# Turning half of x on VectorE and through memory, instead of on TensorE, in the first stage of a fused block on one core

## Chip, core and metric

One core of one Trainium2 chip runs the whole kernel in one launch. The metric is the device time of that core in microseconds (us), the median of several runs. TensorE (PE) is the matrix engine, VectorE (DVE), ScalarE (ACT) and GpSimd (POOL) are the other compute engines, and SyncE (SP) issues the kernel's DMAs.

## What is computed

The reference is one block: a normalised input goes into gated linear attention with 32 heads and 8 groups of keys and values, and behind that stands a small feed-forward part. What matters here is the start:

```
x = L0_attn_hidden_states                                # 4 batches x 512 tokens x 512
h = _layernorm(x, axis=-1)
q = (h @ Wq.T).reshape(B, L, H, D)
k = (h @ Wk.T).reshape(B, L, KVH, D)
v = (h @ Wv.T).reshape(B, L, KVH, D)
...
dt = jax.nn.softplus(h @ Win.T + dt_bias)
```

Every product contracts over the 512 features. TensorE contracts over the partitions, and x arrives with its tokens there, so each normalised tile of 128 tokens by 512 features has to be turned once, so that its features lie on the partitions. Float32 products are made of three passes, high by high, high by low and low by high, so each turned tile is also split into a high and a low part.

## The kernel before

The program has three stages. The change is in the first, `norm_stage`, which takes the first 130 us of the span. There are 16 tiles of 128 tokens, numbered i, four to a batch. `n_xin` holds them all, `n_xn` has three slots (`NORM_SLOTS`) of normalised tiles, and `n_pt` two banks of PSUM that take a turned tile, tile i in bank i % 2. The parts of the turned x stay in `shared`, for the whole program, the high part (index 0) beside the low one (index 1).

For each tile, the engines do this, all in an order written by hand, one in-order list for each engine:

- DVE: `normalise(i)` (L312) writes `n_xn`. It waits until TensorE has turned the tile three before it (`xt_done`). `low_part(i)` (L317) subtracts the saved high part from the bank and writes the low part.
- PE: `turn(i)` (L466) is four transposes of 128 by 128, by the identity, into `n_pt`. `values(v)` (L88, here with outputs `p_tok` and `p_kept`) makes the values of tile v, 12 matmuls of 128x512, and `dt_rows(b)` (L477) is 12 more for each batch, into `n_pdt`. `values(v)` waits for the low part of its tile and for the copy of the tile of values two before it (`v_set`), since there are two banks.
- ACT: `halves(i)` (L391) copies the bank into the high part, and `save_v(v)` (L403) copies a tile of values out of PSUM. The weights' high parts (L395) stand between them, those of the second half of Wv behind `halves(9)` and those of Wk behind `halves(11)`.
- SP: after the loads come `store_v(v)` (L216) for each tile of values, to `v_scratch` in HBM, each waiting for `save_v(v)`. The loads of the first group of Wq (L241) stand behind the eighth of them.

PE's loop over i has `turn(i)`, then `values(i - 2)`, and `dt_rows` behind the values of tiles 3, 7 and 11. After the loop come the values of tile 14, the last `dt_rows` and the values of tile 15, and then those of the second half of Wv (16 and on). ACT's loop is `halves(i)`, then weights if any, then `save_v(i - 2)`. DVE's loop from tile 4 on is `normalise(i)`, `low_part(i - 1)`, with the statistics of four tiles before `normalise` at i = 6 and 10.

The stage ends with decay tables, the first keys and queries, and more values; none of that is moved.

Of the kernel before, what the change touches and what calls it, by code (L numbers as in the profile page):

```python
# [25 lines left out]
ALU = mybir.AluOpType  # L26
# [5 lines left out]
P = 128  # L32
# [87 lines left out]
def norm_stage(nc, io, keep):  # L120
# [7 lines left out]
    with ExitStack() as ctx:  # L128
# [45 lines left out]
        const_set, acol_set = sem("n_const_set"), sem("n_acol_set")  # L174
# [4 lines left out]
        gg_set, G_set, wexp_set, eg_set = sem("n_gg_set"), sem("n_G_set"), sem("n_wexp_set"), sem("n_eg_set")  # L179
        dt_set, dt_up_set, ln_dt_set, ln_dt_min = sem("n_dt_set"), sem("n_dt_up_set"), sem("n_ln_dt_set"), sem("n_ln_dt_min")  # L180
        row_set = [sem(f"n_row_set{k}") for k in range(TAB)]
# [9 lines left out]

        TABLES = 4

        V_LAG, TABLES_AT = 2, 10

# [12 lines left out]
        def _(sp):  # L208
# [87 lines left out]
        def _(dve):  # L296
# [11 lines left out]
            def normalise(i):  # L308
                dve.wait_ge(rstd_set, 1 + next(j for j, (c0, c1) in enumerate(TOGETHER) if i < c1))
                if i >= NORM_SLOTS:  # L310
                    dve.wait_ge(xt_done, i - NORM_SLOTS + 1)
                dve.tensor_scalar(xn[:, i % NORM_SLOTS, :], xin[:, i, :], mv[:, i, 0:1], rstd[:, i:i + 1],  # L312
                                  ALU.subtract, ALU.mult).then_inc(xn_set, 1)

            def low_part(i):
                dve.wait_ge(xt_saved, i + 1)
                dve.tensor_tensor(x_part(1, i), pt[i % 2][:, :, :], x_part(0, i).bitcast(F32), ALU.subtract).then_inc(lo_set, 1)  # L317
# [27 lines left out]
            for i in range(NC, NT):  # L345
# [3 lines left out]
                low_part(i - 1)  # L349
            low_part(NT - 1)  # L350
# [16 lines left out]
            dve.wait_ge(acol_set, 1)  # L367
            dve.tensor_scalar(gg[:, :], dt[:, :], hcol[:, 2:3], -1.0, ALU.mult, ALU.mult).then_inc(gg_set, 1)
            dve.wait_ge(gg_set, 1)
# [9 lines left out]
            dve.tensor_tensor(rows[T_BIAS][:, :], ln_dt[:, :], G[:, :], ALU.subtract).then_inc(row_set[T_BIAS], 1)  # L379
            dve.wait_ge(wexp_set, 1)  # L380
            dve.tensor_tensor(rows[T_W][:, :], dt[:, :], wexp[:, :], ALU.mult).then_inc(row_set[T_W], 1)
# [5 lines left out]
        def _(act):  # L387
            def halves(i):

                act.wait_ge(xt_done, i + 1)  # L390
                act.activation(x_part(0, i), pt[i % 2][:, :, :], ACT.Copy).then_inc(xt_saved, 1)  # L391
# [5 lines left out]
            def save_v(v):  # L397
# [3 lines left out]
                if v in (NT - 2, NT - 1, NT, NT + 1):  # L401
                    act.wait_ge(xt_done, NT)
                act.activation(v_place(v), pv[v % 2][:, :], ACT.Copy).then_inc(v_set, 1)  # L403

            for i in range(NT):
# [9 lines left out]
                if i == 11:  # L415
                    w_high(wk, 0, k_in, 16)
                    act.wait_ge(small_in, 16 * 2 * B)
                    act.activation(hcol[:, 2:3], hcol[:, 1:2], ACT.Exp).then_inc(acol_set, 1)
# [1565 lines left out]
```

## Time and profile before

| | us |
|---|---|
| median of 3 runs | 1765.15 (1765.02 to 1765.41) |
| the profiled execution, its own time | 1765.26 |
| its span | 1763.4 |
| TensorE busy | 1738.6 (99%) |
| VectorE, GpSimd, ScalarE busy | 1271.4, 851.6, 715.1 |
| TensorE, VectorE, ScalarE, GpSimd busy from 20 to 40 us | 20.0, 10.4, 6.8, 3.2 |
| the same from 40 to 60 us | 20.0, 7.1, 7.4, 7.5 |
| share of the 16 DMA engines busy from 20 to 40 and 40 to 60 us | 0.44, 0.43 |

In the rows below a start is in us from the start of the span, the second number is the duration, and the brackets hold the idle time of the engine just before, with what ended it. Matmuls are pipelined, so the distance from one start to the next says what one costs, and not its duration. What lies outside the span (1765.26 less 1763.4) is 1.9 us.

### The profile page before, as it was taken

The numbers are of one execution on the slowest core, as the hardware profiler recorded it, in microseconds if no ns is written. First come the engines' busy times: TensorE is split into PE (matmuls) and PEld (weight loads), VectorE is DVE, ScalarE is ACT, GpSimd is POOL, SyncE is SP. The second block draws the span as 40 slices with busy tenths as digits, with TensorE's granted clock in tenths as the row PEclk, the third lists the DMA queues.
The fourth block names the chain that finished last, engine by engine and source line by source line (L and its number), as shares of the span: only waits on it lengthen the run. The fifth ranks groups of instructions, "written<-read, shape, count | busy, mean of one in ns | idle before, by whom it ended". The sixth has DMA issues, their size and how long they took to land. (4 is left out here: it accounts for less than half of the span.)

```text
span 1763.4 us, 27984 instructions
## 1 busy us (share of the span) xinstructions
PE 1738.6 (99%) x8744; PEld 1468.0 (83%) x8744; DVE 1271.4 (72%) x2353; ACT 715.1 (41%) x2232; POOL 851.6 (48%) x862
## 2 busy tenths in 40 slices
PE   7999999999999999999999999999999999999998
PEld 6788888888888888888888888888778888888886
DVE  5327899998989989889999998998864333333332
ACT  3424444444455444544445444544652212121111
POOL 3126676667667666767666666766401101010101
PEclk9999999999999999999999999999999999999999
DMA  6235323433433333332433333333572323232321
GB/s 208 91 100 146 91 73 118 116 93 112 120 87 118 118 86 111 114 102 77 118 117 90 111 120 88 118 88 105 195 253 76 99 78 102 76 103 74 104 73 47
DMA packets 145985, 190.31 MB, mean 108 GB/s; under 512 B 9136, under 2 KB 79792, under 8 KB 145840
## 3 DMA queue, kind: packets, MB, share of 16 engines
q1 hardware_dynamic: 145840, 188.58, 35.6%
q8 instruction: 66, 1.08, 0.3%
q14 instruction: 79, 0.65, 0.2%
HBM read 141.89 MB, written 46.66 MB: 107 GB/s over the span
## 5 line engine op out<-in xcount | busy, mean ns | idle before, releaser
L117 POOL TENSOR_TENSOR q<-raw_wo_early 128x512 f32<-128x512 f32 x128 | 165.3, 1291 | 195.8 <-DVE raw_wo_early L109 195.6
L88 PE MATMUL p_proj<-shared,wq_hi 128*128 128x512 f32 x744 | 244.5, 389 | 0.0
L1135 ACT ACTIVATE square<-p_y 128x128 f32<-128x128 f32 x512 | 134.2, 277 | 220.1 <-PE p_y L849 218.7
L1877 POOL TENSOR_TENSOR var<-mv,eps 128x1 f32<-128x1 f32 x16 | 3.0, 190 | 402.6 <-DVE mv L1727 402.6
L849 PE MATMUL p_y<-v_tok,probs 128*128 128x128 f32 x1024 | 183.0, 276 | 0.0
L1007 DVE SCALAR_TENSOR_TENSOR z<-p_y,srstd,gate 128x128 f32<-128x128 f32 x512 | 143.7, 343 | 51.6 <-issue 34.5
L1110 ACT ACTIVATE probs<-g_row,stab 128x128 f32<-128x128 f32 x512 | 164.3, 407 | 24.2 <-POOL g_row L1244 24.1
L88 PE MATMUL p_kept<-wg_hi,shared 128*128 128x512 f32 x560 | 173.1, 390 | 0.0
L1258 POOL TENSOR_TENSOR xw_lo<-xw_raw,xw_hi 128x512 fp32r<-128x512 f32 x96 | 131.0, 1364 | 86.0 <-ACT xw_hi L1151 86.0
L88 PEld LDWEIGHTS p_proj<-shared,wq_hi 128*128 128x128 f32 x744 | 139.7, 188 | 30.4 <-DVE raw_wo_early L109 1.2
L1266 POOL TENSOR_TENSOR srstd<-svar,mhalf 128x4 f32<-128x4 f32 x128 | 157.7, 1232 | 10.0
L88 PE MATMUL p_proj<-wg_hi,shared 128*128 128x512 f32 x528 | 162.5, 389 | 0.0
L849 PEld LDWEIGHTS p_y<-v_tok,probs 128*128 128x128 f32 x1024 | 151.0, 193 | 2.5
L848 PE MATMUL p_y<-state,qs 128*128 128x128 f32 x768 | 149.3, 276 | 2.3 <-DVE qs L972 2.3
L88 PE MATMUL p_proj<-shared,wq_lo 128*128 128x512 f32 x372 | 144.8, 389 | 0.0
L1409 DVE TENSOR_TENSOR wq_lo<-w_raw,wq_hi 128x1024 fp32r<-128x1024 f32 x62 | 75.8, 1223 | 83.8 <-ACT wq_hi L1404 83.8
L848 PEld LDWEIGHTS p_y<-state,qs 128*128 128x128 f32 x768 | 122.0, 193 | 7.9 <-issue 3.0
L88 PEld LDWEIGHTS p_kept<-wg_hi,shared 128*128 128x128 f32 x560 | 104.6, 188 | 21.4
L1151 ACT ACTIVATE xw_hi<-xw_raw 128x512 fp32r<-128x512 f32 x96 | 60.7, 632 | 151.7 <-POOL xw_raw L1254 125.3
L88 PEld LDWEIGHTS p_proj<-wg_hi,shared 128*128 128x128 f32 x528 | 99.1, 188 | 21.0
L1254 POOL TENSOR_TENSOR xw_raw<-v_tok,stab 128x512 f32<-128x512 f32 x96 | 110.0, 1146 | 0.1
L88 PE MATMUL p_kept<-wg_lo,shared 128*128 128x512 f32 x280 | 109.1, 390 | 0.0
(244 smaller groups left out, 4395.3 us busy)
## 6 DMA issues: line engine op xcount, KB each, us to landing
g_row<-g_scratch SPq DMA_DIRECT2D x128, 256.0 KB, 5.1
z_scratch<-z_st SPq DMA_DIRECT2D x256, 128.0 KB
w_raw<-z_scratch SPq DMA_DIRECT2D x62, 512.0 KB, 6.7
e_row<-e_scratch SPq DMA_DIRECT2D x96, 256.0 KB, 4.1
w_raw<-in_wq_t SPq DMA_DIRECT2D x16, 512.0 KB, 7.3
w_raw<-in_wg_t SPq DMA_DIRECT2D x16, 512.0 KB, 5.6
v_tok<-v_scratch SPq DMA_DIRECT2D x32, 256.0 KB, 2.9
v_scratch<-n_xin SPq DMA_DIRECT2D x20, 256.0 KB, 2.3
```

The lines of the kernel that those rows point to most:

```text
L88: mm = pe.matmul(out, lhs[a], rhs[e], start=(i == 0 and j == 0), stop=(i == len(pairs) - 1 and j == 2))
L117: pool.tensor_tensor(out, keep["rope_a"][:, s, :], keep["rope_b"][:, s, :], ALU.add).then_inc(keep["roped"], 1)
L848: pe.matmul(p_y[c % 2][:, h, :], qs[:, h, :], state[:, c % 2, h, :], start=True, stop=False)
L849: mm = pe.matmul(p_y[c % 2][:, h, :], probs[:, c % 2, h, :], v_tok[:, b % 2, c, :], start=(c == 0), stop=True)
L1007: zz = dve.scalar_tensor_tensor(z[:, h, :], p_y[c % 2][:, h, :], srstd[:, c, h:h + 1], gate[:, c % 2, h * D:(h + 1) * D], ALU.mult, ALU.mult)
L1110: e = act.activation(probs[:, c % 2, h, :], g_row[:, c % 2, h, :], ACT.Exp, bias=stab[:, b % 2, c, T_BIAS, h:h + 1])
L1135: s = act.activation(square[:, h, :], p_y[c % 2][:, h, :], ACT.Square, scale=2.0 / float(np.sqrt(D)), accum_out=ssum[:, c, h:h + 1])
L1151: act.activation(xw[0][:, :, :], xw_raw[:, :, :], ACT.Copy).then_inc(xw_hi_set, 1)
L1254: pool.tensor_tensor(xw_raw[:, :, :], v, w, ALU.mult).then_inc(xw_raw_set, 1)
L1258: pool.tensor_tensor(xw[1][:, :, :], xw_raw[:, :, :], xw[0][:, :, :].bitcast(F32), ALU.subtract).then_inc(xw_set, 1)
L1266: pool.tensor_tensor(srstd[:, c, :], svar[:, c, :], mhalf[:, :], ALU.pow).then_inc(srstd_set, 1)
L1409: dve.tensor_tensor(by_half(keep["z_lo"][slot]), raw_z(keep, raw_slot), by_half(keep["z_hi"][slot].bitcast(F32)), ALU.subtract).then_inc(k ...
```

## The change

Tiles 8 to 15 (batches 2 and 3) are not turned by TensorE. For them:

- DVE normalises the tile into the PSUM bank `n_pt` instead of `n_xn` and then turns each of its 4 by 16 blocks of 32x32 in place with one instruction, from the bank into `n_xn` (`dve.transpose`).
- SP stores the tile to a new buffer in HBM, `xt_scratch`, with four DMAs of 64 KB (`store_blocks`), one for each band of 32 partitions. Here the blocks change places. Each DMA has 512 pieces of 128 bytes.
- SP then waits for these stores and loads the whole tile, 256 KB in 512 pieces of 512 bytes (`load_turned`), into the place of the low part of x in `shared`.
- ACT's `halves(i)` waits for that load and reads there. DVE's `low_part(i)` reads there and writes there. It stands three tiles behind `normalise` in DVE's list (`BLOCKS_LAG`), and no longer one.

The rest of the diff joins semaphores (`acol_set`, `gg_set`, the `row_set` pair here, and three in the last stage into `max_set`); the waits stand at the same places.

```diff
+        BY_PE = 2 * NC
+        def x_raw(i):
+            b, c = i // NC, i % NC
+            return keep["raw_shared"][:, b * KT:(b + 1) * KT, 1, c * P:(c + 1) * P]
+        def x_whole(i):
+            return pt[i % 2][:, :, :] if i < BY_PE else x_raw(i)
...
+            BLOCKS_AT = 5
+            def store_blocks(i):
+                sp.wait_ge(blocks_set, i - BY_PE + 1)
+                for a in range(P // BL):
+                    sp.dma_start(xt_dram[i].rearrange("(b j) t -> j b t", j=BL)[:, :, a * BL:(a + 1) * BL],
+                                 xn[a * BL:(a + 1) * BL, i % NORM_SLOTS, :].rearrange("j (b t) -> j b t", t=BL)).then_inc(blocks_out, 16)
+            def load_turned(i):
+                sp.wait_ge(blocks_out, 16 * (P // BL) * (i - BY_PE + 1))
+                if i >= BY_PE + 2:
+                    sp.wait_ge(xt_saved, i - 1)
+                sp.dma_start(x_raw(i), xt_dram[i].rearrange("(k p) t -> p k t", p=P)).then_inc(xt_in[i % 2], 16)
...
-            for v in range(8):
+            for v in range(BLOCKS_AT):
                 store_v(v)
+            for i in range(BY_PE, NT):
+                store_blocks(i)
+                store_v(BLOCKS_AT + i - BY_PE)
+                load_turned(i)
             sp.wait_ge(w_lo, 2)
             for i in (1, 2):
                 sp.dma_start(part(w_raw, i), half_piece(io["wq_t"], 0, i)).then_inc(q_in, 16)
-            for v in range(8, NT + TABLES):
+            for v in range(BLOCKS_AT + NT - BY_PE, NT + TABLES):
                 store_v(v)
...
             def normalise(i):
                 dve.wait_ge(rstd_set, 1 + next(j for j, (c0, c1) in enumerate(TOGETHER) if i < c1))
-                if i >= NORM_SLOTS:
-                    dve.wait_ge(xt_done, i - NORM_SLOTS + 1)
-                dve.tensor_scalar(xn[:, i % NORM_SLOTS, :], xin[:, i, :], mv[:, i, 0:1], rstd[:, i:i + 1],
-                                  ALU.subtract, ALU.mult).then_inc(xn_set, 1)
+                before = i - NORM_SLOTS
+                if before >= BY_PE:
+                    dve.wait_ge(blocks_out, 16 * (P // BL) * (before - BY_PE + 1))
+                elif before >= 0:
+                    dve.wait_ge(xt_done, before + 1)
+                if BY_PE <= i < BY_PE + 2:
+                    dve.wait_ge(lo_set, i - 1)
+                elif i >= BY_PE:
+                    dve.wait_ge(blocks_set, i - 1 - BY_PE)
+                into = xn[:, i % NORM_SLOTS, :] if i < BY_PE else pt[i % 2][:, :, :].rearrange("p k t -> p (k t)")
+                dve.tensor_scalar(into, xin[:, i, :], mv[:, i, 0:1], rstd[:, i:i + 1], ALU.subtract, ALU.mult).then_inc(xn_set, 1)
+                if i >= BY_PE:
+                    dve.wait_ge(xn_set, i + 1)
+                    dve.transpose(xn[:, i % NORM_SLOTS, :], into).then_inc(blocks_set, 1)
...
-                low_part(i - 1)
-            low_part(NT - 1)
+                if i <= BY_PE:
+                    low_part(i - 1)
+                elif i >= BY_PE + BLOCKS_LAG:
+                    low_part(i - BLOCKS_LAG)
+            for i in range(NT - BLOCKS_LAG, NT):
+                low_part(i)
...
             def halves(i):
 
-                act.wait_ge(xt_done, i + 1)
-                act.activation(x_part(0, i), pt[i % 2][:, :, :], ACT.Copy).then_inc(xt_saved, 1)
+                if i < BY_PE:
+                    act.wait_ge(xt_done, i + 1)
+                else:
+                    act.wait_ge(xt_in[i % 2], 16 * ((i - BY_PE) // 2 + 1))
+                act.activation(x_part(0, i), x_whole(i), ACT.Copy).then_inc(xt_saved, 1)
...
                 if v in (NT - 2, NT - 1, NT, NT + 1):
-                    act.wait_ge(xt_done, NT)
+                    act.wait_ge(blocks_out, 16 * (P // BL) * (NT - BY_PE))
...
             for i in range(NT):
-                turn(i)
+                if i < BY_PE:
+                    turn(i)
                 if i >= V_LAG:
                     values(i - V_LAG)
```

SP's list before, from the first store of values to the loads of Wq (`x8` is eight such DMAs in a row, each with its wait):

```order
L236 DMA w_raw<-in_wv_t 128x2x512
L216 DMA v_scratch<-n_xin 128x4x128 [waits v_set] x8
L241 DMA w_raw<-in_wq_t 128x2x512 [waits n_w_lo]
L241 DMA w_raw<-in_wq_t 128x2x512
L216 DMA v_scratch<-n_xin 128x4x128 [waits v_set] x6
```

SP's list in the change, from the same place, the first two of the eight rounds:

```order
L268 DMA w_raw<-in_wv_t 128x2x512
L231 DMA v_scratch<-n_xin 128x4x128 [waits v_set] x5
L241 DMA xt_scratch<-n_xn 32x16x32 [waits n_blocks_set]
L241 DMA xt_scratch<-n_xn 32x16x32 x3
L231 DMA v_scratch<-n_xin 128x4x128 [waits v_set]
L249 DMA raw_shared<-xt_scratch 128x4x128 [waits n_blocks_out]
L241 DMA xt_scratch<-n_xn 32x16x32 [waits n_blocks_set]
L241 DMA xt_scratch<-n_xn 32x16x32 x3
L231 DMA v_scratch<-n_xin 128x4x128 [waits v_set]
L249 DMA raw_shared<-xt_scratch 128x4x128 [waits n_blocks_out]
```

Each round puts five new DMAs around one store of values, and the Wq loads now stand behind the eighth round instead of behind the eighth store of values.

ACT's list before, from `halves(8)` on (L391 is `halves`, L403 `save_v`, L395 a weight's high part):

```order
L391 ACTIVATE shared<-n_pt 128x4x128 [waits n_xt_done]
L403 ACTIVATE n_xin<-p_tok 128x512 [waits v_done]
L391 ACTIVATE shared<-n_pt 128x4x128 [waits n_xt_done]
L395 ACTIVATE n_wv_hi<-w_raw 128x1024 [waits n_wv_in] x2
L403 ACTIVATE n_xin<-p_kept 128x512 [waits v_done]
L391 ACTIVATE shared<-n_pt 128x4x128 [waits n_xt_done]
```

The same place in the change (L444 is `halves`, L456 `save_v`, L448 a weight's high part):

```order
L444 ACTIVATE shared<-raw_shared 128x4x128 [waits n_xt_in0]
L456 ACTIVATE n_xin<-p_tok 128x512 [waits v_done]
L444 ACTIVATE shared<-raw_shared 128x4x128 [waits n_xt_in1]
L448 ACTIVATE n_wv_hi<-w_raw 128x1024 [waits n_wv_in] x2
L456 ACTIVATE n_xin<-p_kept 128x512 [waits v_done]
L444 ACTIVATE shared<-raw_shared 128x4x128 [waits n_xt_in0]
```

The instructions stand in the same order; what `halves` waits for has changed from TensorE to a load (`n_xt_in0`, `n_xt_in1`).

## Rows read from the trace of the kernel before

**Rows 1.** Waits of TensorE, whole span: waited for, us in total, times, longest.
```profile
PE n_pt L466 <- DVE n_xn L312: 9.3, 3, 6.6
PE p_tok L88 <- ACT n_xn L403: 0.3, 1, 0.3
```

**Rows 2.** Timeline of TensorE: tile 8 turned, a value tile, `dt_rows`, two value tiles.
```profile
35.40 0.60 PE L466 MATMUL n_pt<-ident,n_xn 128*128 128x128 f32 x4
35.75 0.70 PE L88 MATMUL p_tok<-wg_hi,shared 128*128 128x512 f32 x2
...
69.22 0.39 PE L477 MATMUL n_pdt<-shared,n_win_hi 128*128 128x512 f32 x1
...
72.00 0.62 PE L88 MATMUL p_kept<-wg_hi,shared 128*128 128x512 f32 x2
...
74.75 0.63 PE L88 MATMUL p_tok<-n_wv_hi,shared 128*128 128x512 f32 x2
```

**Rows 3.** Timeline of ScalarE, from `save_v(4)` to the high part of Wk.
```profile
32.38 0.60 ACT L403 ACTIVATE n_xin<-p_tok 128x512 f32<-128x512 f32 x1 [2.17 <-PE p_tok L88]
...
35.59 0.60 ACT L403 ACTIVATE n_xin<-p_kept 128x512 f32<-128x512 f32 x1 [2.13 <-PE p_kept L88]
...
39.28 0.59 ACT L391 ACTIVATE shared<-n_pt 128x512 fp32r<-128x512 f32 x1
39.76 2.01 ACT L395 ACTIVATE n_wv_hi<-w_raw 128x1024 fp32r<-128x1024 f32 x2
...
48.92 0.64 ACT L395 ACTIVATE wk_hi<-w_raw 128x512 fp32r<-128x512 f32 x1
```

**Rows 4.** DMA issues on SP's queue: issue time in ns, minimum, median, maximum.
```profile
L216 SPq DMA_DIRECT2D v_scratch<-n_xin x20: 372/372/837, 17.4 to 104.4; - x20
L223 SPq DMA_DIRECT2D n_win_raw<-in_win_t x1: 469/469/469, 3.6 to 3.6; - x1
```

**Rows 5.** From issue to landing: first the loads of `v_tok`, then two of 0 to 130 us.
```profile
DMA to landing us min/median/max: 2.7/2.9/7.0
...
v_scratch<-n_xin SPq DMA_DIRECT2D x20, 256.0 KB, 2.3
...
w_raw<-in_wq_t SPq DMA_DIRECT2D x2, 512.0 KB, 4.0
```

**Rows 6.** Timeline of VectorE (two rows), then the block transposes up to 175 us.
```profile
33.50 0.69 DVE L317 TENSOR_TENSOR shared<-n_pt,shared 128x512 fp32r<-128x512 f32 x1 [2.10 <-ACT shared L391]
...
37.32 2.46 DVE L303 BATCH_NORM_STATS2 n_stats<-n_xin 128x6 f32<-128x512 f32 x4
...
L1016 DVE STREAM_TRANSPOSE z_st<-z 128x512 f32<-128x512 f32 x3 | 2.1, 711 | 0.1
```

**Rows 7.** DMA from 70 to 76, 10 to 14, and 8 to 12 us.
```profile
q1 hardware_dynamic: 528, 0.26, 14.1%
...
DMA packets 814, 1.59 MB, mean 397 GB/s; under 512 B 39, under 2 KB 39, under 8 KB 814
q1 hardware_dynamic: 814, 1.59, 104.8%
...
DMA packets 1245, 1.48 MB, mean 371 GB/s; under 512 B 552, under 2 KB 552, under 8 KB 1245
q1 hardware_dynamic: 1245, 1.48, 102.6%
```

**Rows 8.** TensorE at the stage's start (PEclk 1.00), and behind a wait of 1.87 us.
```profile
12.00:13.00 1.00, 0.98 (x4) 0.58 (x3) 1.00 (x2) 0.38 (x1) 0.00 (x0) 1.00 1.06 397
...
14.05 1.05 PE L88 MATMUL p_tok<-wg_hi,shared 128*128 128x512 f32 x2
14.90 0.52 PE L88 MATMUL p_tok<-wg_lo,shared 128*128 128x512 f32 x1
...
1291.81 0.47 PE L1453 MATMUL p_tok<-shared,wq_hi 128*128 128x512 f32 x1 [1.87 <-PEq L534]
1292.12 0.40 PE L1453 MATMUL p_tok<-shared,wq_lo 128*128 128x512 f32 x1
```

More of the change, by code:

```diff
@@ L178, in norm_stage @@
             "pre", "ex", "u1", "df", "rc", "ln", "log"))
-        gg_set, G_set, wexp_set, eg_set = sem("n_gg_set"), sem("n_G_set"), sem("n_wexp_set"), sem("n_eg_set")
+        G_set, wexp_set, eg_set = sem("n_G_set"), sem("n_wexp_set"), sem("n_eg_set")
         dt_set, dt_up_set, ln_dt_set, ln_dt_min = sem("n_dt_set"), sem("n_dt_up_set"), sem("n_ln_dt_set"), sem("n_ln_dt_min")
-        row_set = [sem(f"n_row_set{k}") for k in range(TAB)]
+        row_set = sem("n_row_set")
+        blocks_set, blocks_out, xt_in = sem("n_blocks_set"), sem("n_blocks_out"), [sem(f"n_xt_in{i}") for i in range(2)]
         tabs_done, tabs_saved, g_out = sem("n_tabs_done"), sem("n_tabs_saved"), sem("n_g_out")
@@ L366, in _ @@
             dve.tensor_scalar(dt_up[:, :], dt[:, :], LEAST_DT, None, ALU.max).then_inc(dt_up_set, 1)
[L367 to L369 removed]
+            dve.wait_ge(pre_set, 1)
+            dve.tensor_scalar(gg[:, :], dt[:, :], hcol[:, 2:3], -1.0, ALU.mult, ALU.mult).then_inc(dt_set, 1)
+            dve.wait_ge(dt_set, 2)
             for c in range(NC):
@@ L378, in _ @@
             dve.wait_ge(ln_dt_min, 1)
-            dve.tensor_tensor(rows[T_BIAS][:, :], ln_dt[:, :], G[:, :], ALU.subtract).then_inc(row_set[T_BIAS], 1)
+            dve.tensor_tensor(rows[T_BIAS][:, :], ln_dt[:, :], G[:, :], ALU.subtract).then_inc(row_set, 1)
             dve.wait_ge(wexp_set, 1)
-            dve.tensor_tensor(rows[T_W][:, :], dt[:, :], wexp[:, :], ALU.mult).then_inc(row_set[T_W], 1)
+            dve.tensor_tensor(rows[T_W][:, :], dt[:, :], wexp[:, :], ALU.mult).then_inc(row_set, 1)
             dve.wait_ge(trig_in, 32)
@@ L417, in _ @@
                     act.wait_ge(small_in, 16 * 2 * B)
-                    act.activation(hcol[:, 2:3], hcol[:, 1:2], ACT.Exp).then_inc(acol_set, 1)
+                    act.activation(hcol[:, 2:3], hcol[:, 1:2], ACT.Exp).then_inc(pre_set, 1)
                 if i >= V_LAG:
@@ L1499, in output_stage @@
             "x1_set", "x1b_set", "stats_set", "mv_set", "var_set", "rstd_set", "xn_set"))
-        xt_done, qk_done, keys_saved, prod_set, sc_set, mx_set, nmx_set, ew_set = (sem(s) for s in (
-            "xt_done", "qk_done", "keys_saved", "prod_set", "sc_set", "mx_set", "nmx_set", "ew_set"))
+        xt_done, qk_done, keys_saved, prod_set, max_set, ew_set = (sem(s) for s in (
+            "xt_done", "qk_done", "keys_saved", "prod_set", "max_set", "ew_set"))
         rden_set, hwn_set, hwt_done, hwt_saved, f_done, res_set, c_set = (sem(s) for s in (
@@ L1742, in weigh @@
                 dve.wait_ge(prod_set, i + 1)
-                dve.tensor_reduce(sc[:, :], qk, AX.X, ALU.add).then_inc(sc_set, 1)
-                dve.wait_ge(sc_set, i + 1)
-                dve.reduce_max(mx[:, :], sc[:, :], AX.X).then_inc(mx_set, 1)
-                dve.wait_ge(mx_set, i + 1)
-                dve.tensor_scalar(nmx[:, :], mx[:, :], -SCALE, None, ALU.mult).then_inc(nmx_set, 1)
+                dve.tensor_reduce(sc[:, :], qk, AX.X, ALU.add).then_inc(max_set, 1)
+                dve.wait_ge(max_set, 3 * i + 1)
+                dve.reduce_max(mx[:, :], sc[:, :], AX.X).then_inc(max_set, 1)
+                dve.wait_ge(max_set, 3 * i + 2)
+                dve.tensor_scalar(nmx[:, :], mx[:, :], -SCALE, None, ALU.mult).then_inc(max_set, 1)
                 dve.wait_ge(ew_set, i + 1)
```

13 lines of the change are left out of this document (8 added, 5 removed).

## The prediction, made before the change was run

> **What bounds the kernel now.** I began with the page's busy times, then went to TensorE's waits, then to the timelines of the first 80 us, engine by engine, and last to the times of the DMAs. TensorE is the bound: it is busy for 1738.6 of 1763.4 us, and its longest wait by far is for the first normalised tiles at the very start [rows 1]. Behind 12.6 us the stage that the change touches has one wait of 0.3 us on TensorE [rows 1]. So each microsecond taken from TensorE's list there comes off the time, and each microsecond for which TensorE stands still there goes onto it; nothing behind it is loose enough to absorb one. The reader should see in [rows 2] that TensorE's steps touch each other: a tile's turn costs 35.75 - 35.40 = 0.35 us, a tile of values 74.75 - 72.00 = 2.75 (others take up to 2.84; I use 2.8 on average), and `dt_rows` 72.00 - 69.22 = 2.78.
>
> **What it removes.** Eight turns leave TensorE: 8 x 0.35 = 2.8 us [rows 2]. That is the whole gain, 0.16% of the time, and less than the 0.2% (3.5 us) that a measurement of this kernel can tell from no change.
>
> **The beat that TensorE asks for.** Over four tiles TensorE would now want 4 x 2.8 + 2.78 = 14.0 us, or 3.5 us a tile. Before, each engine could follow at that beat, because a tile became ready 0.6 us of ACT and 0.69 us of DVE behind its turn. Now a tile is ready when it has been to memory and back, so the question is the beat at which such tiles arrive.
>
> **The round that the change closes.** Three in-order lists bind one another. SP issues `load_turned(i)` behind `store_v(i - 3)`. That store waits for `save_v(i - 3)` on ACT. In ACT's list `save_v(i - 3)` stands behind `halves(i - 1)`. And `halves(i - 1)` now waits for the load of tile i - 1. So the load of a tile can't be issued before the load of the tile before it has landed, was copied, and a copy of values and a store issue have followed. Its length is:
> - issue to landing of a 256 KB load in pieces of 512 bytes: the trace has 32 such loads (`v_tok`), 2.7 at least and 2.9 in the median [rows 5]. Here each stands right behind a 256 KB store, whose data take 0.85 us of all 16 engines (14.1% of 6 us) [rows 7], 0.4 us after it. Up to 0.4 us of that is still ahead. I take half of it: 3.1 us.
> - `halves` to the next instruction on ACT 39.76 - 39.28 = 0.48, and `save_v` 0.60 [rows 3]
> - the store's issue 0.37 [rows 4], and 0.1 for three hops between engines (0.02 to 0.05 each, as starts follow ends in these timelines)
>
> Together 3.1 + 0.48 + 0.60 + 0.37 + 0.11 = 4.66 us, against the 3.5 that TensorE wants. Two rounds are longer, since weights stand between `halves` and `save_v`: 1.95 us at tile 9 and 0.64 at tile 11 [rows 3]. That is the core of the forecast: the tiles come 1.1 us a tile too slowly.
>
> **Where it begins and ends.** `save_v(4)` ends at 32.38 + 0.60 = 32.98 [rows 3], so SP starts the four stores of tile 8 at 33.4 (the tile itself is turned on DVE by 32.4: normalise and 0.71 us [rows 6]). An issue of a 64 KB DMA with 512 small pieces takes 0.47 [rows 4], so the last is issued at 34.8 and lands at some 36.6 to 37.1 (2.3 us, with 256 KB, is the nearest landing [rows 5]). `store_v(5)` is issued by 36.6 (35.59 + 0.60 + 0.37 [rows 3, 4]). So the first load goes out at 36.7. Its tile is ready at 36.7 + 3.1 + 1.4 = 41.2, with TensorE due at tile 8 at 35.40 + 2 x 2.8 + 2.78 = 43.8: the head start is 2.6 us. The last goes out at 36.7 + 7 x 4.66 + 1.95 + 0.64 = 71.9 and lands at 75.0. With the two copies (0.60 and 0.69) and the hops, the low part of tile 15 is there at 76.4. The last `dt_rows` waits for it, 79.2, and the values of tile 15 end at 81.9. Before they end at 74.75 [rows 2]. The sum is **+7.2 us**; TensorE's stalls, from the values of tile 9 to the last `dt_rows`, sum to 2.8 + 7.2 = 10.0 us, at most some 2 us each.
>
> **What hides the rest.** DVE gets 8 x 0.71 = 5.7 us of block transposes [rows 6], and a write to and a read from PSUM where there was SBUF. Its cover is the wait of 2.1 us at each tile [rows 6]. The batch of statistics (2.46 us) now stands ahead of tiles 10 and 11, and `low_part(8)` behind those, at 41.7, still 2 us early. Cost nothing; without that cover it would be some 0.7 us a tile. The loads of Wq go out at 72.3 instead of 46.45, behind eight rounds. They land 4.0 us after their issue [rows 5], near 77, and ACT waits there with `save_v(15)` behind it, which isn't possible before 81.9 anyway: nothing. The chain of the decay tables moves as a whole with the last `dt_rows`. The joined semaphores put no wait in a new place: nothing.
>
> **The unknown cost: stores in pieces of 128 bytes.** No row before has one. What the rows give is two sizes. Of 512 bytes, written: 0.141 x 6 x 16 / 512 = 26 ns of one engine each. Of 2 KB, read: 1.048 x 4 x 16 / 775 = 87 ns [rows 7]. The line through them comes to 11.5 ns at 128 bytes. And from 8 to 12 us, with 552 small packets among 693 large ones, 65.7 - 59.9 leaves 5.8 us or 10 to 11 ns for each small one, most of them the 128-byte pieces of a load [rows 7]. At 11.5 ns a 64 KB store takes 0.37 us, less than its issue. The four stores of a tile then land at 0.41 + 1.41 + 1.8 = 3.6 us behind the load before them, and the round of 4.66 hides them. They decide from 1.86 + 0.2 + 4S = 4.66 on, S = 0.65 us a store, which is 20 ns a piece. I take the low value, because it is the one read from pieces of that size, though in the other direction.
>
> The Trainium skill has a rule against this change (DMA: Bandwidth & Descriptors, Specifications): below 512 bytes a DMA engine does a read-modify-write. In this trace small pieces that are read from memory show no such price, with 11 ns each, and no run here shows one that is written.
>
> **Rivals.**
> 1. *The stores are the round.* If a 128-byte piece costs what one of 512 costs (26 ns), S is 0.85, and the four stores land 5.5 us behind the load before: 0.41 + 1.45 + 3.4, and 0.2 behind the load's own data. The round is 5.5 but for 6.6 at tile 9, 39.6 us in all instead of 35.2, and the first load is 1.4 late: +7.2 + 4.4 + 1.4 = +13.0 us, 1778. For it: the direction of those 11 ns, and that stores write into a place of 128 bytes in each row of 512. Against it: the line through two sizes.
> 2. *The stores cost twice that*, each piece a read and a write of 512 bytes. S is 1.7, the round 0.41 + 1.45 + 6.8 + 0.2 = 8.9, seven of them 62, the first load 4.8 late: +39 us, 1804. By the skill's rule above this is what would happen.
> 3. *TensorE falls to its slower pace in the stalls.* The first matmuls of the stage stand 0.43 us apart (14.05 to 14.90, two of them) and not 0.23, though the granted clock in their row reads 1.00, the upper level of 2.4 GHz; ahead of them TensorE had waited three times [rows 8, 1]. At 12 x 0.43 = 5.1 us a tile TensorE would be slower than the round; nine such steps from 47.4 on end at 93.4: +18.6, 1784. Against it: behind a wait of 1.87 us the next two stand 0.31 apart, near full pace [rows 8], and the stalls here are no longer, with 2.8 us of matmuls between two.
> 4. *Faster: the round is short enough.* It decides at the landing. Each 0.1 us of it counts eight times, 0.8 us. With 2.9 the sum is +5.6, with 2.7 it is +4.0, with the 2.3 of the stores of the same size +0.8, and at 2.2 it crosses zero. From 1.8 on TensorE never waits, and the time is 1765.3 - 2.8 = 1762.5. No load of 256 KB lands that soon [rows 5].
>
> **How the numbers follow.** The sum is made against the profiled execution: 1765.26 + 7.2 = 1772.5. That stands 0.1 above the median of the runs, so the forecast is 1772.4. Its own range is a landing from 2.7 to 3.7 (the second adds all of the store's data and a little of those queued behind): +4.0 to +12, 1769 to 1777. Chances: this forecast 0.70, of which little lies below 2.7; rival 1 0.14; rival 2 0.05; rival 3 0.05; rival 4 with all that ends within 3.5 us 0.06, half of it faster or near it. The range of 8 in 10 reaches over rival 1 and a little below the forecast's own end, and leaves out rivals 2 to 4: 1768 to 1781. Slower by over 0.2% is the forecast and rivals 1 to 3: 0.93. Within 0.2%: 0.04. Faster: 0.03.
>
> **What would show it.** In the changed kernel's profile: no transposes on TensorE behind the eighth tile; loads of `raw_shared` on SP's queue, 4.6 us apart from the second on, with 6.6 once; ACT's `halves` of tiles 9 to 15 waiting for a DMA; TensorE waiting for DVE's low part or ACT's copy of values, six or seven times, 1 to 2 us each, 10 us in all, from the values of tile 9 to the last `dt_rows`. Loads landing well under 2.7 us, or SP held by the four stores (`blocks_out`) and not by the copy of values, would prove the size wrong. No stalls at all, because ACT or SP don't stand in the order I read, would prove the mechanism wrong.

## The result: 16.9 us slower, in two places

| | before | changed |
|---|---|---|
| median of 5 runs, us | 1765.41 (1765.02 to 1767.6) | 1782.34 (1781.69 to 1783.83) |
| span of the profiled execution | 1763.4 | 1779.6 |
| start of the first matmul on `n_wv_hi` behind tile 15 | 74.75 | 86.51 |
| `save_k` of the first head group's first step, later by | | 11.8 |
| the same in the last group, later by | | 16.2 |

The ratio is 1.0095, with a 95% interval of 1.0081 to 1.0108. It is slower, as forecast, but by 16.9 us and not by 7.2, and 1.3 us beyond the upper end of the range. In the spans the difference is 16.2 us, and it falls in two lumps: **11.8 us** before the values of tile 16, where the change was made, and **4.4 us** in the second stage, in five steps of 0.8 to 1.1 us, where nothing was changed.

**The first stage.** TensorE's waits over the whole span (waited for, us in total, times, longest); [rows 1] is the same view of before:

```profile
PE n_pt L519 <- DVE n_xn L356: 9.3, 2, 7.1
PE p_kept L88 <- ACT n_xin L456: 5.1, 2, 2.7
...
PE p_proj L88 <- DVE raw_wo_early L109: 3.1, 5, 0.8
PE p_tok L88 <- DVE shared L363: 2.5, 2, 2.1
...
PE p_kept L88 <- DVE shared L363: 1.3, 1, 1.3
```

The wait at the very start is the same 9.3. New are the three lines with `n_xin L456` (the copy of values) and `shared L363` (the low part), 8.9 us in all, and the one with `p_proj`, which belongs to the second stage. From the last group to the program's end nothing more is lost on balance: the later start is 16.2 us there and the spans differ by 16.2. (In between some 2 us are gained and lost again, the loss at 1308 us in a wait of 3.55 us where it was 1.87 before [rows 8].)

TensorE's timeline, its rows with idle time before them, places the first stage's waits (start, duration, what runs, idle and releaser). These answer [rows 2], where nothing waited:

```profile
49.24 1.19 PE L88 MATMUL p_kept<-wg_hi,shared 128*128 128x512 f32 x2 [2.72 <-ACT n_xin L456]
54.26 0.74 PE L88 MATMUL p_tok<-wg_hi,shared 128*128 128x512 f32 x2 [0.45 <-DVE shared L363]
59.72 1.19 PE L88 MATMUL p_kept<-wg_hi,shared 128*128 128x512 f32 x2 [2.41 <-ACT n_xin L456]
...
70.98 0.73 PE L88 MATMUL p_kept<-wg_hi,shared 128*128 128x512 f32 x2 [1.28 <-DVE shared L363]
76.10 0.89 PE L88 MATMUL p_tok<-wg_hi,shared 128*128 128x512 f32 x2 [2.10 <-DVE shared L363]
80.87 0.51 PE L530 MATMUL n_pdt<-shared,n_win_hi 128*128 128x512 f32 x1 [0.16 <-DVE shared L363]
```

Six waits, 9.1 us in all, from the values of tile 9 to the last `dt_rows`, as the prediction placed them. ScalarE at tiles 8 and 9 answers [rows 3]; `halves` (L444) now waits for the load, and the copy of values (L456) stands behind it, once with Wv between:

```profile
41.06 0.63 ACT L444 ACTIVATE shared<-raw_shared 128x512 fp32r<-128x512 f32 x1 [4.86 <-DMA raw_shared<-xt_scratch]
41.60 0.58 ACT L456 ACTIVATE n_xin<-p_tok 128x512 f32<-128x512 f32 x1
46.09 0.63 ACT L444 ACTIVATE shared<-raw_shared 128x512 fp32r<-128x512 f32 x1 [3.91 <-DMA raw_shared<-xt_scratch]
46.63 1.99 ACT L448 ACTIVATE n_wv_hi<-w_raw 128x1024 fp32r<-128x1024 f32 x2
48.52 0.58 ACT L456 ACTIVATE n_xin<-p_kept 128x512 f32<-128x512 f32 x1
```

SyncE's timeline shows the beat (start and length of the issue). L249 is `load_turned`, L241 `store_blocks`, L231 `store_v`:

```profile
33.46 2.19 SPq L241 DMA_DIRECT2D xt_scratch<-n_xn  x4
...
38.28 0.38 SPq L249 DMA_DIRECT2D raw_shared<-xt_scratch  x1
38.70 2.19 SPq L241 DMA_DIRECT2D xt_scratch<-n_xn  x4
...
42.73 0.42 SPq L249 DMA_DIRECT2D raw_shared<-xt_scratch  x1
...
64.87 0.45 SPq L249 DMA_DIRECT2D raw_shared<-xt_scratch  x1
65.38 3.40 SPq L241 DMA_DIRECT2D xt_scratch<-n_xn  x4
...
71.63 0.38 SPq L249 DMA_DIRECT2D raw_shared<-xt_scratch  x1
```

The eight loads go out 4.45, 6.90, 4.85, 5.61, 4.78, 6.76 and 4.69 us apart. The issue times (ns: minimum, median, maximum) and landings that answer [rows 4, 5], first of the block stores, then of the loads, and SyncE's one wait for the block stores:

```profile
L241 SPq DMA_DIRECT2D xt_scratch<-n_xn x32: 488/549/1591, 33.5 to 73.8; - x32
...
DMA to landing us min/median/max: 2.3/2.6/3.6
...
L249 SPq DMA_DIRECT2D raw_shared<-xt_scratch x8: 376/446/453, 38.3 to 76.3; - x8
...
DMA to landing us min/median/max: 2.8/3.2/4.7
...
SPq L249 <- DMA xt_scratch<-n_xn: 1.6, 1, 1.6
```

On VectorE, which answers [rows 6], a tile's normalising into PSUM takes 0.81 us (0.54 into SBUF before) and its block transpose 0.72. From 68 to 70 us nearly all DMA packets are pieces of the block stores (this answers [rows 7]); their share of 16 engines gives 0.704 x 2 x 16 / 1630 = 14 ns a piece:

```profile
DMA packets 1630, 0.22 MB, mean 110 GB/s; under 512 B 1584, under 2 KB 1630, under 8 KB 1630
...
q1 hardware_dynamic: 1630, 0.22, 70.4%
```

TensorE's granted clock, for [rows 8]. The columns are the window's length, busy time of PE, PEld, DVE, ACT and POOL, granted clock, DMA share and GB/s.

```profile
50.00:55.00 5.00, 4.55 (x15) 3.31 (x14) 1.28 (x2) 1.12 (x2) 2.44 (x2) 0.74 0.75 160
55.00:60.00 5.00, 2.59 (x11) 1.84 (x11) 2.22 (x4) 1.72 (x4) 0.93 (x1) 0.94 0.75 154
60.00:65.00 5.00, 5.00 (x17) 3.92 (x17) 1.64 (x3) 1.11 (x2) 0.35 (x1) 0.71 0.74 157
65.00:70.00 5.00, 4.70 (x21) 3.51 (x19) 0.00 (x0) 0.43 (x1) 0.00 (x0) 1.00 0.76 160
...
75.00:80.00 5.00, 3.90 (x10) 3.10 (x11) 0.69 (x1) 1.34 (x4) 0.00 (x0) 0.66 0.75 204
```

Behind the three longest waits, 2.72, 2.41 and 2.10 us, the granted clock is 0.74, 0.71 and 0.66 in the mean, that is, partly at the lower of its two levels (1.2 and 2.4 GHz). A tile of values then takes longer: from 49.24 to 53.81 (54.26 less the 0.45 of idle) is 4.57 us, and the two others took 4.30 and 4.61, where 2.8 is the rule. So the 11.8 us lost and the 2.8 of the turns that are gone are made up of 9.1 us of waits, some 5 us of slower pace in these three tiles, and 0.1 or 0.2 in each of some others. What the slower pace is worth by itself is another question, answered with the rivals below.

**The second stage.** VectorE's waits with releaser "issue" between two steps of its loop over the groups of heads. First of the changed kernel (from 140 to 1270 us), then the same wait before:

```profile
DVE probs L1019 <- issue: 18.0, 5, 4.0
```

```profile
DVE probs L965 <- issue: 1.2, 5, 0.5
```

The timeline of VectorE at one of the five, the first instruction behind the jump, in the changed kernel and then before:

```profile
441.24 0.69 DVE L1019 TENSOR_TENSOR probs<-p_score,probs 128x512 f32<-128x512 f32 x1 [3.34 <-issue]
```

```profile
426.56 0.69 DVE L965 TENSOR_TENSOR probs<-p_score,probs 128x512 f32<-128x512 f32 x1 [0.45 <-issue]
```

The second stage handles eight groups: the first and the last are written out, and six go through a loop, so there are five jumps back. At each jump VectorE stands for 3.1 to 4.0 us before the first instruction of the loop that keeps it busy, and not 0.2 to 0.5. Most of it is caught up, but part reaches TensorE, which waits for `raw_wo_early` five times (3.1 us in the table above). The group behind each jump starts later by 0.8 us three times, 0.9 once and 1.1 once, which makes the 4.4 us. The loop's 384 instructions are the same in both kernels. What differs is where they stand in VectorE's list: in front of them are now 449 instructions and not 441, by the eight block transposes.

The changed kernel's trace also shows what such a wait ends with. The loop's first two instructions, which VectorE's sequencer handles alone, come at 437.9 and 438.0 us, as soon as the step before is done; the third is the one that comes at 441.24. And at 439.50 one packet of instructions, of 8 KB, starts on a DMA engine:

```profile
L1018 DVEq EVENT_SEMAPHORE  x1: 21/21/21, 438.0 to 438.0; - x1
...
q14 instruction: 1, 0.01, 3.9%
```

At all five jumps VectorE goes on 1.72 to 1.74 us behind the start of such a packet, whether it waited 3.1 us or 4.0. Before the change, packets of this size start at like distances behind the branch (1.0, 2.3 to 3.9 and 4.3 to 4.8 us), and VectorE goes on at 3.0 to 3.3 us, ahead of the last of them. So the wait ends with the arrival of instructions, of which as many packets stand around the jump as before. That is read from the times; no run moved the packets.

### The profile page after: what moved, and what is told of

Its sections match the earlier page's. It is cut to its first block and busy times, and to the rows that moved or that the text cites. A ratio compares the mean times of both kernels' runs of the same rounds, so it can differ in the third digit from the quotient of the medians.

```text
span 1779.6 us, 27990 instructions
## 1 busy us (share of the span) xinstructions
PE 1742.2 (98%) x8712; PEld 1467.6 (82%) x8712; DVE 1273.1 (72%) x2361; ACT 714.9 (40%) x2232; POOL 849.1 (48%) x862
## 5 line engine op out<-in xcount | busy, mean ns | idle before, releaser
L1019 DVE TENSOR_TENSOR probs<-p_score,probs 128x512 f32<-128x512 f32 x128 | 87.8, 686 | 37.1 <-PE p_score L88 18.2
```

The source lines that it names most:

```text
L1019: dve.tensor_tensor(probs[:, c % 2], p_score[:, :, :], probs[:, c % 2], ALU.mult).then_inc(probs_set, 1)
```

## The experiments

Each expectation was written before its runs. Shifts are how much later than in the kernel before the second stage's first `save_k` starts, in the profiled execution. Two kernels with the first stage of before, in experiment 1, stand there at 0.0 and -1.5, so a difference in shift of 1.5 us between two executions says nothing by itself.

**1. Does the place of VectorE's loop cost 4 us by itself?** The kernel before, with eight one-element instructions ahead of the loop and nothing else:

```diff
+            for j in range(8):
+                dve.memset(spare[:, j:j + 1], 0.0)
             dve.wait_ge(trig_in, 32)
```

> The kernel before, with eight one-element writes more in VectorE's list, in the idle time of the first stage ahead of the first rotation; nothing else is changed. In the changed kernel's trace VectorE stands still for 3.3 us or so at the head of its loop over the groups, five times, where it stands for 0.45 us before, and TensorE loses 0.8 us each time; the two lists differ by exactly eight instructions ahead of the loop. Theory A (the place of the loop in VectorE's list): the same five waits of over 3 us come here, and the time is +4 us, 1769.5. Theory B (it comes from the new traffic, the new buffer in memory or the later start of the second stage): no such waits, and within 1 us of before.

Measured: 1769.87 against 1765.59, ratio 1.0023 (1.0013 to 1.0033). The wait is there, and TensorE's with it:

```profile
DVE probs L968 <- issue: 17.9, 5, 4.1
...
PE p_proj L88 <- DVE raw_wo_early L109: 3.4, 5, 0.9
```

With four instructions and not eight (`range(4)`):

> The kernel before with four one-element writes more in VectorE's list instead of eight. Theory A says that some place between none and eight is where the waits at the loop's head jump from 0.3 to over 3 us; this run says on which side four is: +4 us with five waits of over 3 us, or as before.

1764.74, a single run, with that wait at 1.2 us for all five, as before. So the edge lies between 445 and 449 instructions ahead of the loop.

**2. The same from the other side.** The changed kernel without eight waits of VectorE that others make superfluous (one, for constants, is moved), so that 441 instructions stand ahead of the loop again:

```diff
-                dve.wait_ge(rstd_set, 1 + next(j for j, (c0, c1) in enumerate(TOGETHER) if i < c1))
+                if i not in (3, 5, 6, 7, 9, 10, 11, 13, 14, 15):
+                    dve.wait_ge(rstd_set, 1 + next(j for j, (c0, c1) in enumerate(TOGETHER) if i < c1))
...
-                elif before >= 0:
-                    dve.wait_ge(xt_done, before + 1)
```

> The changed kernel without eight separate wait instructions in VectorE's list of the first stage, all of them implied by waits that stay; so VectorE's loop over the groups stands at the same place in its list as before the change. Theory A (place of the loop): the five waits of 3.3 us at the loop's head shrink to those of before, TensorE's five waits of 0.6 to 0.8 us in the second stage are gone, the first stage is as in the changed kernel, and the time falls by 4 us, to 1778. Rival (the eight added writes of e1_before_8more cost something else, or any change of the list does): the waits stay, 1782.

1776.42, ratio 1.0059 (1.0042 to 1.0076). The wait is gone, and the shift stays at 12.3 us from the stage's first step to its last:

```profile
DVE probs L1019 <- issue: 1.3, 5, 0.5
```

The median is 5.9 us below the changed kernel's, the span 4.4, and the four runs lie between 1773.49 and 1779.57; 1778 was expected. These three settle the second lump: it is the loop's place, in either kernel, whatever fills the list ahead of it. A further run tried a rule for the place, 128 instructions more (`range(128)`, in the changed kernel):

> The changed kernel with 128 one-element writes more in VectorE's list, at the place of e1_before_8more. Theory A, in the form that the code is brought in blocks of 256 instructions and a loop of 384 has to lie in two of them: 128 more put its head into the first half of a block again, the waits at the loop's head fall from 3.3 to about 0.5 us, and the time falls by 4 us, to about 1778, with the first stage as it is. If any longer list only makes it worse, or the traffic is the cause: no change, 1782.

1780.82, ratio 1.009 (1.0073 to 1.0107), and `DVE probs L1022 <- issue: 18.8, 5, 4.2`. With 577 ahead it is as bad as with 449, and not 4 us better, so that rule fell. The Trainium skill (Runtime: NRT & Kernel Launch, Instruction fetch mechanics) says that a taken branch to a target outside the pages held forces a fetch of that page before execution goes on. The waits at the jumps fit that in kind. The Trainium skill's blocks of 256 instructions, counted from the start of the list, don't tell 445 from 449: in both the loop reaches from the second such block into the fourth. The packets at the jumps are of 8 KB, half of the 16 KB that the Trainium skill gives to such a block. Counted in halves, of 128 instructions, 449 and 577 stand at the same place in their block, which would fit that 128 more changed nothing. That is an estimate from the figures of the Trainium skill; what sets the edge between 445 and 449 was not tested.

**3. Do the block stores cost by their 128-byte pieces?** The changed kernel with stores of the same size to whole rows, in pieces of 512 bytes. The blocks don't change places there, which leaves that part of the computation out:

```diff
-                    sp.dma_start(xt_dram[i].rearrange("(b j) t -> j b t", j=BL)[:, :, a * BL:(a + 1) * BL],
-                                 xn[a * BL:(a + 1) * BL, i % NORM_SLOTS, :].rearrange("j (b t) -> j b t", t=BL)).then_inc(blocks_out, 16)
+                    sp.dma_start(xt_dram[i, a * P:(a + 1) * P, :].rearrange("(j k) t -> j k t", k=KT),
+                                 xn[a * BL:(a + 1) * BL, i % NORM_SLOTS, :].rearrange("j (k t) -> j k t", t=P)).then_inc(blocks_out, 16)
```

> The changed kernel with its four stores of 64 KB made in 128 pieces of 512 bytes instead of 512 of 128; the blocks of x don't change places then, so this part of the computation is left out. The ScalarE round theory: the stores were hidden in all rounds but the first, where SyncE waited 1.7 us for them; loads 4.6 to 4.8 us apart as before, the time 1 to 3 us less, about 1780. If the 128-byte pieces are what makes the tiles late (DMA engines full, loads and stores of values held up behind them): loads near 4 us apart or less, the time 5 us less or more, under 1777.

1782.25, ratio 1.0096 (1.0079 to 1.0113): the changed kernel's time, and not the 1 to 3 us less that were expected. The issues are shorter and the landings sooner, and only the first load profits, by 0.9 us; the intervals between the loads are those of the changed kernel, 4.5 to 6.9:

```profile
L241 SPq DMA_DIRECT2D xt_scratch<-n_xn x32: 421/427/2363, 33.6 to 72.6; - x32
...
DMA to landing us min/median/max: 1.7/2.2/3.9
```

**4. Which list binds the round?** Two edits, alone and together. On ScalarE, the copy of values ahead of `halves`, so that it no longer waits for a load:

```diff
             for i in range(NT):
+                if i >= BY_PE:
+                    save_v(i - V_LAG)
                 halves(i)
...
-                if i >= V_LAG:
+                if V_LAG <= i < BY_PE:
                     save_v(i - V_LAG)
```

> The changed kernel, with save_v(i - 2) ahead of halves(i) in ScalarE's list for tiles 8 to 15. If the round through ScalarE is all that holds the tiles back, the first stage loses its stalls: the loads follow at TensorE's 3.5 us, and the time falls by 10 us or more, to about 1771. If SyncE's own round (load, four stores, their landing, next load), which the trace puts at 4.45 us between the first two loads, stands right behind it, every round is 4.4 to 4.8 us, the two longer ones (6.9 and 5.6) too, and the time falls by only 3 to 5 us, to about 1778.

On SyncE, the stores of the next tile ahead of this tile's load (`blocks_out` becomes two semaphores, by turns):

```diff
+            store_blocks(BY_PE)
             for i in range(BY_PE, NT):
-                store_blocks(i)
+                if i + 1 < NT:
+                    store_blocks(i + 1)
                 store_v(BLOCKS_AT + i - BY_PE)
                 load_turned(i)
```

> The changed kernel with SP's order alone altered: the stores of tile i+1 go out ahead of the load of tile i, with two semaphores. ScalarE's order stays. If the round through ScalarE's copy of values is the one that binds (load, high part, copy of values, store of values, load), as predicted, this alone gives little: loads 4.6 to 4.9 us apart, the second stage 11 to 12 us later, 1781 to 1783. If the stores of the blocks were what binds (each tile's stores behind the load before), the loads come 4.2 or less apart and the time falls to 1777 or less. With the run that changed ScalarE's order alone (7.8 us of shift left) and the one with both (2.7) this is the fourth corner.

And both:

> As e2_copy_first, and in SyncE's list the four stores of tile i + 1 stand ahead of the load of tile i (with one semaphore for even and one for odd tiles). Both rounds are broken. The rounds theory: loads 3.5 us apart, TensorE's stalls between 40 and 90 us under 2 us in all, the first stage ends no later than before, and what stays above before is the 4 us of the second stage less up to 2.8 us of turns: 1767 to 1769. The rival, that stores of 128-byte pieces are dear in themselves: the 16 DMA engines are full, loads stay over 4 us apart, and the time is over 1773.

| | time, us | ratio (95%) | shift | loads apart, us |
|---|---|---|---|---|
| changed kernel | 1782.34 | 1.0095 (1.0081, 1.0108) | 11.8 | 4.5 to 6.9 |
| SyncE's order alone | 1782.63 | 1.0095 (1.008, 1.0111) | 13.2 | 4.6 to 6.8 |
| ScalarE's order alone | 1777.1 | 1.0064 (1.0047, 1.0081) | 7.8 | 4.3 to 6.4 |
| both | 1772.48 | 1.0038 (1.0024, 1.0053) | 2.7 | 3.4 to 5.1 |

The round through ScalarE's copy of values is the one that binds, as predicted: moving the block stores alone brings nothing. With it opened, the next one, SyncE waiting for its own block stores, stands right behind at 4.3 to 4.7 us, but for one interval of 6.4. SyncE's waits with ScalarE's order alone changed:

```profile
SPq L249 <- DMA xt_scratch<-n_xn: 11.7, 8, 3.2
```

Only with both open does the first stage lose little. Its 1772.48 lies above the 1767 to 1769 that were expected for the rounds alone and just under the 1773 of dear stores; experiment 5 finds what is left.

**5. Are the two losses separate?** Both orders and the eight waits left out:

> e3_both_rounds with the same eight wait instructions less. If the two losses are independent and are all there is, it is 1772.5 - 4.2 = 1768.3, still 2 to 3 us above before, with TensorE's stalls at tiles 9 and 10 left. If the first stage's stalls come back when the second stage is quick, or the reverse, over 1770.

1768.89, ratio 1.0019 (1.001 to 1.0029), shift 3.0 and constant through the stage: they add, as far as the runs tell (the loop's place is worth 4.3 us in experiment 1, 5.9 in 2 and 3.6 here). What held most of the 3 us was one wait of TensorE of 2.54 us at 53.61, for `low_part(10)`, and the slower pace behind it: the values of tile 10 took 4.44 us. I had blamed the statistics that stand ahead of tile 10 on VectorE (with the length of `low_part(10)` beside GpSimd as the rival) and moved them to where VectorE waits:

```diff
-                if i % NC == 2 and i + 2 < NT:
-                    statistics(range(i + 2, i + 2 + NC))
+                if i == 6:
+                    statistics(range(8, 12))
                 normalise(i)
+                if i == 7:
+                    statistics(range(12, 16))
```

> The kernel with both rounds shortened and VectorE's eight waits left out, and one more edit: the statistics of tiles 12 to 15 (2.7 us on VectorE) move from ahead of the normalising of tile 10 to right behind the normalising of tile 7, where VectorE waited 4.3 us. In the run without this edit TensorE still stood still 0.75 us at 48.05 and 2.54 us at 53.61, both for a low part of VectorE, and low_part(10) there took 2.29 us instead of 0.69. If the place of the statistics is what makes the tiles late there, both stalls go, the shift of the second stage falls from 3.0 us to about 0 (the two stalls less nothing), and the time is about 1766, 0.2% at most above the kernel before. If it is the length of low_part(10), beside GpSimd's work on Wv, the second stall stays at about 1.6 us or more wherever the statistics stand, and the time is 1767 to 1769. A time under 1763.5 would need all stalls gone and the gain of the eight turns kept; I give that 1 in 10.

1768.69, ratio 1.0016 (1.0007 to 1.0025), and the same wait at the same time: the statistics were not it. This kernel's rows of VectorE and GpSimd say what was:

```profile
47.31 0.69 DVE L366 TENSOR_TENSOR shared<-raw_shared,shared 128x512 fp32r<-128x512 f32 x1 [1.70 <-ACT shared L448]
...
50.99 2.57 DVE L366 TENSOR_TENSOR shared<-raw_shared,shared 128x512 fp32r<-128x512 f32 x1 [1.52 <-ACT shared L448]
...
48.30 4.71 POOL L299 TENSOR_TENSOR n_wv_lo<-w_raw,n_wv_hi 128x1024 fp32r<-128x1024 f32 x2 [17.50 <-ACT n_wv_hi L452]
```

The same subtraction takes 0.69 us, and 2.57 while GpSimd makes the low parts of Wv: it ends 0.55 us behind them (53.56, 53.01). The same holds for the three other kernels in which it was long (1.63, 2.10 and 2.29 us, each ending 0.55 us behind them). Before the change a low part read one source from PSUM; in the changed kernel both lie in SBUF. So the last edit moves GpSimd's work away, by making the high parts it needs earlier on ScalarE:

```diff
+                if i == BY_PE:
+                    w_high(wk, 0, k_in, 16)
                 halves(i)
...
-                if i == 9:
+                if i == 7:
                     w_high(wv[1], 1, wv_in, 32)
                     w_high(wv[1], 2, wv_in, 32)
                 if i == 11:
-                    w_high(wk, 0, k_in, 16)
```

> The kernel of e9_stats_earlier with one more edit: on ScalarE the two high parts of the second half of Wv stand behind halves(7), where ScalarE waited 2.1 us, and no longer behind halves(9); that of Wk stands ahead of halves(8), where it waited 3.1 us for a load. GpSimd's low parts of Wv (two, 4.7 us in all) so start at about 36.5 us instead of 48.3. In the run without this edit low_part(10) took 2.57 us (50.99 to 53.56) where all other low parts took 0.69, and GpSimd was at work on Wv from 48.30 to 53.01. If VectorE's subtraction with both sources in SBUF is held by GpSimd's work on SBUF, low_part(10) falls to 0.69, TensorE's stall of 2.54 us at 53.61 falls to 0.7 or less, and the second stage moves forward by 2 to 4 us, since TensorE's clock then has less reason to fall (granted 0.71 from 55 to 60 us there): 1764 to 1767. If the length of low_part(10) comes from something else (the DMA traffic, which has a share of 1.03 to 1.04 there), it stays at 2 us or more and the time stays at 1768 to 1769. A time under 1763.5, below the kernel before by more than a measurement is uncertain, needs no stall left at all: 2 in 10.

1765.31 against 1765.72, ratio 0.9999 (0.999 to 1.0008), shift 0.5. The subtraction is back at 0.69, and TensorE's waits there are short. It ends 2.34 us sooner, 1.88 by its length and 0.46 by its start. The DMA traffic, the rival in the expectation, is as dense as it was (a share of 1.01 from 50 to 55 us, and 1.04 without the edit), so it was not that:

```profile
50.53 0.69 DVE L366 TENSOR_TENSOR shared<-raw_shared,shared 128x512 fp32r<-128x512 f32 x1 [1.76 <-ACT shared L448]
...
47.34 0.73 PE L88 MATMUL p_kept<-wg_hi,shared 128*128 128x512 f32 x2 [0.42 <-DVE shared L366]
51.28 0.74 PE L88 MATMUL p_tok<-wg_hi,shared 128*128 128x512 f32 x2 [0.91 <-DVE shared L366]
```

The granted clock is 1.00 from 45 to 60 us here, and the values of tile 10 take 3.06 us and not 4.44: the slower pace was 1.4 us of the 3. So the whole loss can be taken back by order and by the eight waits less, and what is left is no gain either: the 2.4 us of waits that remain eat most of the 2.8 us of the eight turns.

## Why the prediction was right and wrong

**Right: the gain, the mechanism and its place.** The transposes are gone from TensorE behind tile 7. The round through load, high part, copy of values, store and load is what binds (experiment 4), its first step starts at the values of tile 9, and the interval was 4.45 to 4.85 where nothing special stands in it, for a predicted 4.66.

**Wrong by 4.5 us: two terms of the round.** The high part of tile 15 started at 79.46 and not at 75.0. Term by term:

| | predicted | measured | difference |
|---|---|---|---|
| first load goes out | 36.7 | 38.28 | +1.6 |
| seven intervals, but for the sixth | 30.6 | 31.3 | +0.7 |
| the sixth, tile 13 to 14 | 4.66 | 6.76 | +2.1 |
| last landing | 3.1 | 3.1 | 0 |

- *The first load.* I had the four block stores at 0.47 us an issue and 2.3 us of landing, from DMAs of other shapes [rows 4, 5]. They took 0.55 each, and the last was out near 35.1 and done at 38.2, some 3.1 later. (The prediction's own terms give 34.8 + 2.3 = 37.1; it took 36.7.) There is no round yet to hide them there, and SyncE waited 1.6 us. That looks like the rival about the stores, true for one tile of eight, but the price of a piece isn't it: in the four kernels with eight waits fewer the fourth store of tile 8, in the same pieces, landed in 2.0 us, and in the five others with 128-byte pieces in 2.9 to 3.1. In those five a packet of instructions, of 8 KB, starts 1.0 us behind that store's issue, and in the four none does before the store has landed. Whether it is the cause was not tested. The landings of these four stores (minimum, median, maximum), in the changed kernel and with eight waits fewer:

```profile
DMA to landing us min/median/max: 2.3/2.4/3.1
...
DMA to landing us min/median/max: 2.0/2.3/2.4
```

- *The sixth interval.* Its load landed 4.7 us after its issue and the four store issues took 3.40 (rows at 64.87 and 65.38 above), where 3.2 and 2.2 to 2.5 are the rule. From 66 to 68 us the queues show one packet of instructions, of 16 KB, on one of the 16 DMA engines:

```profile
q8 instruction: 1, 0.02, 3.0%
```

The packet and a slow transfer come together in all ten traces with the change, among them the one with 512-byte pieces (64 to 66 us) and the last one (56 to 58, an issue of 1.73 us). That it is the cause was not tested. The trace of before had the sign, and I didn't look for it: the packet stands at 53.2 us, and the store of values issued at 51.8 landed in 4.2 us and not in 2.3. Nothing there waits for a landing, so it cost nothing.

```profile
DMA to landing us min/median/max: 4.2/4.2/4.2
...
q8 instruction: 1, 0.02, 9.2%
```

**Wrong by 4.4 us: what an instruction costs that nobody waits for.** The step that failed is "Cost nothing" of VectorE's eight transposes. Their 0.7 us each were hidden indeed. But they also moved a loop, some 250 us further on, by eight places, and experiments 1 and 2 show that this alone costs the 4.4. "Nothing behind it is loose enough to absorb one" was said of TensorE's time and was true; the place of a loop in a list was in no part of my working.

**The rivals.** That the stores are the round, at 26 ns a piece or twice that: false. A piece of 128 bytes took 14 ns, near the 11.5 that I worked out, and four times longer pieces changed nothing (experiment 3). The Trainium skill's rule (DMA: Bandwidth & Descriptors, Specifications), a read-modify-write below 512 bytes, may hold inside the memory, but at 14 ns a written piece no such price is seen here; by it the time would have been 1804. The slower pace of TensorE: its rows came (0.66 to 0.74 behind the long waits), its price did not. In the run with eight waits fewer the granted clock was 1.00 in every window of 5 us from 45 to 70 (0.74 from 70 to 75), the shift was 12.3 all the same, and TensorE merely waited longer: 1.77 us at tile 10 where it was 0.45. So too at the end: the last `dt_rows` waited 0.16 us behind a slow tile of values in the changed kernel and 1.70 behind one at full pace in the kernel with 512-byte pieces. While the round sets the beat, a slow TensorE only fills its own waits. In the kernels with the round opened (experiment 5) TensorE is the bound again, and there the clock of 0.71 from 55 to 60 us did cost, 1.4 us of their 3.

**Forecast and range.** 7.2 + 4.5 + 4.4 = 16.1, for 16.2 between the spans. The range took in the landing's size and the dearer stores, and left out everything beyond the first stage.

## What to carry to other kernels

Before a resource is called free, follow the in-order lists around the new wait until they close: what a loaded tile's copy stands ahead of decides the beat, and opening one such round shows the next right behind it. Count instructions ahead of a hardware loop as well as time: even on an engine with idle time to spare, eight more of them cost 4.4 us at five jumps, and the view to look at is the wait called "issue" at the loop's first instruction. And where a source moves from PSUM to SBUF, look what GpSimd reads at that moment.

## What the runs showed of the hardware

- A jump back to a loop of 384 instructions on VectorE costs it 0.2 to 0.5 us of standing still with 441 or 445 instructions ahead of the loop, and 3.0 to 4.2 with 449 or 577. In the changed kernel VectorE went on 1.7 us behind the start of an 8-KB packet of instructions, at all five jumps.
- A VectorE subtraction of 128x512 with both sources in SBUF took 1.63 to 2.57 us beside GpSimd's, in four kernels, and ended 0.55 us behind it each time, 0.69 otherwise; with GpSimd's work moved it was 0.69 (experiment 5). The Trainium skill says so (SBUF — State Buffer, SBUF: two separate sides): such an instruction and a GpSimd one that reads SBUF lock each other out for the whole instruction. The trace of before had a like sign, in a normalising of 1.53 us (0.54 otherwise) at 49.67 beside GpSimd's low part of Wk. It has one large source and not two, so what the Trainium skill says of two inputs doesn't cover it:

```profile
49.67 1.53 DVE L312 TENSOR_SCALAR n_xn<-n_xin,n_mv,n_rstd 128x512 f32<-128x512 f32 x1
...
49.63 1.29 POOL L261 TENSOR_TENSOR wk_lo<-w_raw,wk_hi 128x512 fp32r<-128x512 f32 x1 [3.21 <-ACT wk_hi L395]
```

- Stores in pieces of 128 bytes took 14 ns a piece of one DMA engine, their issue 0.55 us, that of the same bytes in pieces of 512 took 0.43.
- Beside a 16-KB packet of instructions on one DMA engine, transfers landed in 3.9 to 5.4 us where 2.3 (stores of values) or 3.2 (loads) is the rule, before the change and with it. The two were only seen together.
- Behind waits of 2.1 to 3.1 us in this stage TensorE's granted clock fell to its lower level for part of the next tile, which then took 4.3 to 4.6 us where 3.0 is the rule behind a wait; but not behind every such wait (2.35 and 2.21 us with eight waits fewer stayed at 1.00).
